# TensorE's order inside the odd half-steps of an attention pipeline

## What is computed

```python
# 1. token pooling, 750 -> 375 tokens
h   = gelu(gelu(x @ W1 + b1) @ W2 + b2)
imp = sigmoid(h @ W3 + b3) + 1e-5; imp = imp / imp.sum(1) * 375; cs = cumsum(imp)
h   = einsum('btn,btc->bnc', Wt, x)              # Wt: overlaps of cs with a grid of 375 cells
# 2. attention, 8 heads of 64, causal, with a distance bias per head
xn  = layernorm(layernorm(h)) * gamma + beta
q,k,v = three-tap filters along the tokens of (w1 @ xn), for wq, wk, wv
attn = softmax(q @ k.T * scale + bias);  h = h + (attn @ v) @ wout.T
# 3. 16 experts, each takes the 375 tokens that score highest for it, and one shared expert
h   = h + experts(layernorm(h)) + shared(layernorm(h))
```

## Time and profile before

| | |
|---|---|
| median of 3 runs | 1337.28 us |
| the profiled execution | 1337.11 us |
| its span, first to last instruction | 1335.4 us |
| mean granted TensorE clock | 0.956 |
| TensorE matmul busy | 1181.6 us, 88% |
| TensorE weight load busy | 992.4 us, 74% |
| VectorE busy | 895.8 us, 67% |
| ScalarE busy | 732.2 us, 55% |
| GpSimd busy | 405.9 us, 30% |

### The profile page before, as it was taken

One profiled execution on the slowest core, in us unless ns is written; L12 is line 12 of the kernel. 1 busy time (PEld: TensorE's weight loads), 2 busy tenths in 40 slices (PEclk: granted clock), 3 DMA queues, 4 the chain that ended last, 5 costly groups with the idle time before them and its releaser, 6 DMA issues. The chain is left out here.

```text
span 1335.4 us, 23186 instructions
## 1 busy us (share of the span) xinstructions
PE 1181.6 (88%) x7812; PEld 992.4 (74%) x7812; DVE 895.8 (67%) x2614; ACT 732.2 (55%) x1845; POOL 405.9 (30%) x379
## 2 busy tenths in 40 slices
PE   6999999999978999999999999999995998766663
PEld 6999999999966777777777777777773777545552
DVE  5656566656658988888888888897874887222220
ACT  2444534344448877788877778887882432222220
POOL 5000001302011444333344323231111001688885
PEclk9999999999989999999999999999997998988876
DMA  5100000000010000000000000000002100444542
GB/s 140 31 13 24 12 24 12 18 19 12 1 36 1 19 18 17 26 26 26 25 19 11 23 27 26 25 11 11 14 16 55 30 18 19 100 91 89 90 87 23
DMA packets 91800, 42.94 MB, mean 32 GB/s; under 512 B 31066, under 2 KB 88007, under 8 KB 91687
## 3 DMA queue, kind: packets, MB, share of 16 engines
q1 hardware_dynamic: 67207, 33.49, 9.3%
q0 software_dynamic: 23808, 6.69, 3.9%
q10 hardware_dynamic: 672, 1.31, 0.3%
HBM read 28.22 MB, written 9.65 MB: 28 GB/s over the span
## 5 line engine op out<-in xcount | busy, mean ns | idle before, releaser
L487 PE MATMUL bank<-h1hl,W2hl 128*128 128x376 f32 x1536 | 277.3, 336 | 2.9 <-DVE h1hl L643 2.9
L487 PEld LDWEIGHTS bank<-h1hl,W2hl 128*128 128x128 f32 x1536 | 263.6, 189 | 7.4 <-issue 4.3
L1057 ACT ACTIVATE P<-P,nmax 125x375 f32<-125x375 f32 (+2 forms) x384 | 189.0, 501 | 1.4 <-DVE nmax L1185 1.4
L587 ACT ACTIVATE h<-bank,b2c 128x375 f32<-128x375 f32 x128 | 73.5, 575 | 207.3 <-PE bank L487 207.3
L226 POOL TENSOR_SCALAR cellmax<-grid,csb 125x375 f32<-125x375 f32 x96 | 122.7, 1288 | 206.0 <-DVE csb L219 133.1
L1185 DVE CUSTOM_DVE_ANT_0 P<-bank,nbias 125x375 f32<-125x375 f32 (+2 forms) x384 | 138.9, 410 | 2.1 <-PE bank L898 1.7
L1067 ACT COPY PT<-bank 128x500 f32<-128x500 f32 (+1 forms) x256 | 127.9, 553 | 6.5 <-PE bank L911 6.1
L898 PE MATMUL bank<-QK 64*125 64x375 f32 (+2 forms) x768 | 116.3, 407 | 4.2 <-DVE nmax L1185 3.7
L911 PE MATMUL bank<-ident,P 125*128 125x125 f32 x768 | 113.4, 275 | 0.6 <-ACT P L1057 0.4
L1075 ACT ACTIVATE tap<-bank,qkd 128x375 f32<-128x375 f32 x128 | 68.6, 571 | 79.2 <-PE bank L951 79.1
L1651 ACT ACTIVATE hE<-bank,EB 128x375 f32<-128x375 f32 x64 | 36.7, 573 | 134.8 <-PE bank L1600 132.0
(11 more groups left out here) (209 smaller groups left out, 2326.7 us busy)
## 6 DMA issues: line engine op xcount, KB each, us to landing
X<-in_x_dram SPq DMA_DIRECT2D x31, 375.0 KB
EW<-in_L_ffn_w_dram SPq DMA_DIRECT2D x32, 256.0 KB
token_table<-row SPq DMA_DIRECT2D x16, 210.9 KB
tTall<-tT SPq DMA_DIRECT2D x16, 187.5 KB, 2.5
out_dram<-oS SPq DMA_DIRECT2D x16, 187.5 KB
tTall<-in_L_tok_W_dram ACTq DMA_DIRECT2D x1, 1024.0 KB, 8.9
EB<-in_L_ffn_b_dram SPq DMA_DIRECT2D x16, 62.5 KB
tok<-token_table,ids POOLq DMA_INDIRECT x48
```

The costliest lines, as they stand in the source:

```text
L487: last = nc.tensor.matmul(bank[4 + m % 2][:, :NE], W2hl[:, a, k, m * 128:(m + 1) * 128], h1hl[:, p, b, k], start=(k == 0 and n == 0), stop ...
L587: nc.scalar.activation(h2[:, p, m], bank[4 + m % 2][:, :N], ACT.Gelu, bias=b2c[:, m:m + 1]).then_inc(s_g2, 1)
L1057: nc.scalar.activation(P[:, 2 * r + q, SEG[i]:SEG[i] + w], P[:, 2 * r + q, SEG[i]:SEG[i] + w], ACT.Exp, bias=nmax[:, 2 * r + q, i:i + 1], ...
```

## The change

In TensorE's body `attend` and `transpose_probs` move up, ahead of `transpose_v` and `project_v`. In an even half-step nothing changes, since `transpose_v` and `project_v` run in odd ones only and `attend` in even ones only. In an odd half-step the order becomes scores, probabilities' transposes, value transposes, value projection. No instruction is added or removed, no wait changes its number, and no other engine's order changes.

```diff
                         if part == 0 and valid(m):
                             project_qk(m, d, m % 2)
+                        k, e = pair_before(b, c, 2)
+                        if part == 0 and valid(k):
+                            attend(k, e, u if c >= 2 else v_)
+                        k, e = pair_before(b, c, 1)
+                        if valid(k):
+                            transpose_probs(k, e, part)
                         if part == 1:
                             if valid(b):
                                 transpose_v(b, c)
                             if valid(m):
                                 project_v(m, d, m % 2)
-                        m, d = pair_before(b, c, 2)
-                        if part == 0 and valid(m):
-                            attend(m, d, u if c >= 2 else v_)
-                        m, d = pair_before(b, c, 1)
-                        if valid(m):
-                            transpose_probs(m, d, part)
```

## The result

The changed kernel takes 1343.72 us (median of 5 runs, 1340.82 to 1346.47) against 1337.28 us: 6.4 us more, ratio 1.0045 with a 95% interval of 1.0029 to 1.0061. Run again beside other kernels it took 1344.74 us against 1338.86 (1.0048, 1.0034 to 1.0061). It is slower, by somewhat less than the 10.4 us forecast.

A forecast was written before the change was run, and what follows sets the result against it. TensorE was taken to bound the body from h1 to h5 and ScalarE from h5 to h1'. 5.4 + 0.7 + 1.0 + 2.1 + 1.4 = 10.6 us on 1337.1 gave 1347.7 us, range 1339 to 1355.

The forecast's parts named there:

- The rule for an odd half-step: With S the start of an odd half-step's scores, value copy at S + 2.31, next `project_qk` not before S + 4.83.
- h3: Half-step h3: the transposes fill TensorE's gap before the value transposes, a gain of 0.31 us.
- h5: Half-step h5: `project_qk` 0.35 us later on TensorE, value copy and later taps 0.58 us later on ScalarE.
- h1': Half-step h1 of the next body: part comes back, the pooling matmuls start only 0.76 us later.
- The 1.20 at h7: Half-step h7: ScalarE's value copy, and its queue up to the taps of h0', 1.20 us later.
- The sum of a body: One body: +0.76 - 0.31 = +0.45 us, over 12 periods +5.4 us.
- the sign of being right: In the profile after, periods of about 39.8 instead of 39.3 us.
- The ends: Last bodies: +1.0 from lag at h1 less h3's gain, +2.1 from `project_qk`, +1.4 from the last h5 and h7.
- The body ahead of the periods: The body before the 12 periods loses only its h7, +0.7 us, bounds 0 and 1.2.
- (a): Rival, chance 0.10: gaps simply filled, gain 0.31 us at h3 and 0.48 at h1, 0.79 a body, 1327 us.
- (b): Rival, chance 0.14: only TensorE's wait for `VT` costs, -0.1 us a body, no change, 1338 us.
- (c): Rival, chance 0.16: handshake costs at h1, h3, h5, or late copies at h5 move VectorE; 0.85 us a body, 1354 us.

The follow-up runs named there:

- e4_h5: New order in half-step h5 of every body only, against the kernel before: 1345.19 us, ratio 1.005.
- e6_last: New order only in bodies b = 14 and 15 and the empty ones behind them, against the kernel before: 1341.89 us, ratio 1.0022.
- e1_h1h3: New order in half-steps h1 and h3 of every body only, against the kernel before: 1326.91 us, ratio 0.9923.
- e7_best: Against the kernel before: new order in h3, and h1 up to b = 13, with VectorE's pTs copy at h1 moved ahead: 1331.45 us, ratio 0.9946.
- e3_act: Changed kernel with ScalarE's q = 1 probability copies ahead of the value copy and tap in odd half-steps: 1338.68 us, ratio 1.0002 against the kernel before.

## Why the prediction was right, and where its sizes were off

**The rule for an odd half-step held.** `project_qk` was put at S + 4.83 and starts at S + 4.81 (h6) and S + 4.82 (h0'). At h0' no wait is listed, since TensorE comes out of its scores only 0.04 us sooner: from their start to that of `project_qk` it is 0.87 us (735.54 to 736.41), before the change 0.83. The value copy was put at S + 2.31 and comes at S + 2.28. h3 gained 0.36 (from the pooling matmuls to the output projection 11.80 us, 704.05 to 715.85, against 12.16) where 0.31 was said.

**h5 had the right value for TensorE and the wrong account for ScalarE.** `project_qk` came 0.33 later, 0.35 was said. But the sentence that from h5 to h1' ScalarE runs without a gap and sets the body is wrong at h7: its taps at h6 do come 0.52 later behind h5's scores (729.30 against 722.94, before 729.26 against 723.42), but at the value copy of h7 it had waited for TensorE, and e4_h5 shows that its lag is not handed on past it. The 1.20 at h7 came out nearly right all the same, because it was worked out from TensorE's scores: 0.33 + (2.28 - 1.46) = 1.15. The taps of h0' in fact come 0.33 + 7.59 - 6.79 = 1.13 later, the two distances being from h7's scores to the taps (731.59 to 739.18, and 731.75 to 738.54). So the lag came by way of TensorE's scores, and the number owes nothing to the one that ScalarE was said to carry: that this part of the account was wrong cost nothing by luck.

**A wait at h0' was not foreseen.** `project_qk` lasts 1.63 instead of 1.30 us, since its second half writes `G1`, from which VectorE must first have read the gate's logits:

```profile
736.70 0.20 DVE L1283 TENSOR_REDUCE lmax<-bank 125x3 f32<-125x48 f32 x1
736.93 0.21 DVE L1286 TENSOR_TENSOR lg<-bank,lmax 125x48 f32<-125x48 f32 x1
```

VectorE takes these behind `VT` and the overlap (L234), which are late: the second of them ends at 737.14, and the weights of the second half are loaded from 737.26 on. Before the change it ended at 736.48, ahead of that half. It cost nothing here: TensorE still idles 0.61 at h1' until the copies come.

**h1' gave back 0.49**, from the taps of h0' to the pooling matmuls (4.45 us, 739.18 to 743.63, against 4.94), where 0.44 was said. The value transposes are part of it: they occupy TensorE for 0.25 when they stand behind other transposes (715.00 to 715.25), against the 0.32 behind scores that was used.

**The sum of a body** was +0.45; the terms as measured give 1.13 - 0.49 - 0.36 = +0.28, and the windows view says +0.26. Three terms were each off by 0.05 to 0.07 and all to the same side; in a difference of larger terms that is over a third of the 0.45. The period that opens at 429.64 was taken to be like the others, but is 38.62 us long and loses 0.64; why it loses more was not traced. With it the 12 periods make 3.5 us instead of 5.4 and their mean is 39.55, where 39.8 was given as the sign of being right.

**The ends.** Forecast 4.5 for what comes behind b = 13's pooling matmuls, measured 4.14; e6_last puts 3.12 of it in b = 14 and 15 (forecast 3.5) and so 1.0 in b = 13 (forecast 1.0). The body ahead of the periods was to lose 0.7. In the second profile of the changed kernel it takes 41.14 us, 5.15 of them the pooling matmuls, before the change 41.26 with 5.57 (388.38 to 393.95, granted clock 0.73 in that stretch); without these matmuls 35.99 against 35.69, so it lost 0.3. The first profile has the low clock in another place of this body (0.73 from 399.23 to 403.23), and e6_last, with the old order there, has 35.69 again.

**From 8.0 to 6.4.** Stage two thus lost 7.7 + 0.3 = 8.0 us, the medians differ by 6.4 and 5.9. Behind the last output projection the changed kernel's profiles are 1.2 and 1.7 us shorter (329.75 and 329.25 against 330.9), and what comes ahead of the first pooling matmuls differs between the profiles by up to 4.4 us (387.23 to 391.59). Why the end would be shorter was not tried and stays open; the executions of other kernels lie between 329.3 and 331.0 there, so one profile each can't tell.

**The rivals.** (a), the gaps are simply filled, describes h1 and h3 (e1_h1h3: -0.82 a body, 0.79 was said), and has the wrong sign for the whole. The Trainium skill ("Perfetto Trace Analysis", Optimization Strategy) would have one find the gaps of the fullest engine and let what they wait for start sooner or end faster. The change does something else, it moves other work into the gaps, so its result does not speak against that rule; e7_best does let an awaited copy start sooner, and there its wait went and the body grew by 0.40 us. (b), only `VT` counts, is what e3_act comes near: with ScalarE's order turned the result is no change. (c) did not happen: the handshake at h1 was in the sum already, and at h3 and h5 the first transposes start 0.84 us behind the scores' start (713.25 to 714.09, 722.94 to 723.78) with no wait listed.

## What to carry to other kernels

When an engine's gap is filled by moving work, the work that it moves past comes later by the length of what was moved (0.85 us here), less the gap that was filled (0.3 at h5, nothing at h7); ask of each place in the period separately who waits for that and where the next long idle stretch (a lump) on its path is. Idle time counted here only where it lay behind the delay: the same move was worth 9.5 us in the two half-steps with a lump behind them and cost 17 us in the two without. Where engines meet in a fixed order, try turning the other engine's order together with the first one's (here 7.0 us of the 7.7 came back), or apply the move only where it pays (here 10.3 us under before); and measure halves of a change before judging the whole.

## What was not expected

Moving a 0.5 us copy ahead on VectorE made the body 0.4 us longer through two other engines (e7_best), though the wait it was aimed at did go. And the runs of the changed kernel spread by up to 5.7 us, while its middle stage, 582.5 us long, is the same within 0.02 us in its two profiles: with a change confined to one stage, marks inside that stage resolve what medians of whole runs can't.
